# Transposes of the identity placed before waits of TensorE in a linear-attention and mixture-of-experts kernel

## The chip, the cores and the metric

The kernel runs on one core of a Trainium2 chip. The metric is the time of one execution on the device, in microseconds (us): the median of three runs of the kernel before is 821.56 us, the runs lie between 821.05 and 823.49 us. The profile is one more execution, taken by the hardware profiler.

## What is computed

The input x has 16 sequences (blocks) of 512 tokens with 128 features. Each passes an attention layer without a softmax, and then a layer of shared and routed experts, cut here to what matters:

```python
q = silu(x @ Wq); k = silu(x @ Wk); v = x @ Wv             # 16 heads of 8
q, k = lrpe(q, theta), lrpe(k, theta)                      # times cos and sin: 16 per head
energy = einsum('bhnd,bhmd->bhnm', q, k) * tril            # causal, no softmax
out = einsum('bhnm,bhmd->bhnd', energy, v) @ Wo
out = layernorm(out * sigmoid(x @ G1 @ G2)) * gamma + beta
x1 = layernorm(x + out)
# router: 2 of 8 experts for each token, at most 1280 tokens an expert
routed = scatter_add(expert(x1[dispatch]) * weight)        # 8 experts, inner size 512
shared = (silu(x1 @ sg) * (x1 @ su)) @ sd                  # inner size 1024
return layernorm(x1 + shared + routed)
```

## The kernel before

The kernel is written with explicit semaphores. Each of the five engines has its own list of instructions, in an order written out by hand, and waits with `need(engine, semaphore, value)` before an instruction. What is queued behind a waiting instruction on the same engine waits too.

Stage 1 (until about 530 us) goes through the 16 blocks. In `step(b, par)` TensorE does the attention of block b and projects the input of block f = b + 1. A block's attention has four parts c of 128 tokens. For each part `energies_and_state(c)` computes q k^T of the 16 heads (L1960) and a partial sum of the state (L1980), and `states_and_out(c)` computes the output of the part before (`from_states` L1920, `attend` L1935). For c = 0 that is the last part of the block before. Between them stand the turning of the input (`input_turned`, L2046), the projections (`project`, L1853 to L1855 by `three`; `values_projected`, L2291 to L2293), the turning of the keys (`keys_turned`, L2069), the output projection (`project_out`, L2261), the turning of x1 (`turn_x1`, L2250), the router's logits (L2270) and positions (L2282 to L2288), and pairs of gate and up products of the shared experts (`shared_gate`, `shared_up`, also through `three`). Blocks -1 to 1 follow `opening` and `first_blocks`, blocks 2 to 11 `with_feed_forward`, blocks 12 to 14 `with_spare_pairs` (12 in an order of its own), block 15 `last_block`. DIRECT and SPARE are 10. `spare_turn` gives s0 = 2, s1 = 3 for block 13 and s0 = 4, s1 = 5 for block 14.

The other engines follow TensorE. ScalarE copies the turned input (`a_xhi`), copies the turned keys out of PB[0] and PB[1] into Kt (L891, semaphore `a_kt`, two for each block) and the attention's output into oT (L810, `a_out`), and computes silu. VectorE masks the energies into EM (L1243, two instructions for each part, `v_mask`) and the states into SM (L1252, `v_S`), multiplies gate and up of the shared experts out of UB (L1273, `v_h`), rotates q and k by the angles (`turn`, L1224 or L1235) and adds the shared experts' sums (`v_xs`). SyncE's queue starts, block by block, sixteen copies of Q by head (`q_by_head`, L292), the load of an input (L418), and in blocks 2 to 11 eight copies that double Q and K (`double`, L442 and L444). GpSimd sends the rows to the experts' slots (L626).

PSUM has eight banks of 512 columns: PB[0], PB[1], SBK and UB (all "bank" in the trace), EB2 (energy_banks) and EG2 (energy_and_gate_banks, of which the second is GB).

Stage 2 (from about 553 us) computes the experts. `step(e, par)` of expert 0 begins with `turn_rows(0, 0, (0, 1))`, which waits for the first expert's rows from DRAM (`e_ldx`) and turns them into PB[0] and PB[1] (L2385). `spread_down(AGAIN, ...)` (L2328) is down projection of the shared experts. Stage 3 is the rest of the shared experts and the last layernorm.

Of the kernel before, what the change touches and what calls it, by code (L numbers as in the profile page):

```python
# [55 lines left out]
def build(nc, x, wqk, wvg, g1t, g2, wo, gamma, beta, theta, rwt, rg, ru, rd, sg, su, sd, out):  # L56
# [3 lines left out]
    with ctx:  # L60
# [191 lines left out]
        def need(eng, s, value):  # L252

            if value > 0:
                eng.wait_ge(s, value)
# [1591 lines left out]
        def _(pe):  # L1847
# [52 lines left out]
            def down_back(q, bank):  # L1900
# [3 lines left out]
                    ins = t.transpose(bank[:, P * c:P * (c + 1)], down_T(q)[:, P * c:P * (c + 1)], ident[:])  # L1904
                ins.then_inc(pe_dT, 1)

            def from_states(b, par, c):

                need(pe, a_out, 4 * b + c)
                need(pe, v_mask, 8 * b + 2 * c + 2)  # L1910
                need(pe, v_S, NS * b + 2 * c + 1)
                cols = slice(T * c, T * (c + 1))
                for crossed in (1, 0):
                    for s in (0, 1):
                        k, j = 2 * c + s, (s + crossed) % 2
                        rows = slice(T * j, T * j + T)
                        for half in (0, 1):
                            if k > 0:
                                o = T * half + 32 * j
                                ins = t.matmul(AV2[o:o + 32, s, cols], SM[rows, k - 1, 32 * half:32 * half + 32],  # L1920
                                               QT[rows, par, c // 2, half, P * (c % 2) + T * s:P * (c % 2) + T * (s + 1)],
                                               start=True, stop=False)
                    if crossed:
                        ins.then_inc(pe_sm, 1)
# [15 lines left out]
            def step(b, par):  # L1940
# [78 lines left out]
                def states_and_out(c):  # L2019

                    if c > 0 and core:
                        from_states(b, par, c - 1)
                    elif c == 0 and back:
                        from_states(b - 1, 1 - par, 3)
                    if core:
                        state(c, 0)
                    if c == 1 and shared_turn(b - 1) is not None:
                        down_back(shared_turn(b - 1), UB)
                    if c > 0 and core:
                        attend(b, par, c - 1)  # L2030
                    elif c == 0 and back:
                        attend(b - 1, 1 - par, 3)
# [121 lines left out]
                def with_spare_pairs():  # L2154

                    s0, s1 = spare_turn(b, 0), spare_turn(b, 1)
                    if b == DIRECT + 2:
                        states_and_out(0)
                        down_by_column(shared_turn(b - 1), range(3))
                        input_turned()  # L2160
                        energies_and_state(0)
                        down_by_column(shared_turn(b - 1), range(3, 8))
                    else:
                        input_turned()
                        states_and_out(0)
                        shared_pair(s0, SPARE)
                        energies_and_state(0)
                    project(f, 0)
                    if b == DIRECT + 2:
                        turn_x1(b, par)  # L2170
                        states_and_out(1)
                        project(f, 1)
                        project_out(b)
                        energies_and_state(1)
                        logits(b)
                        states_and_out(2)
                        shared_pair(s0, SPARE)
                        project(f, 2)
                        project(f, 3)
                        energies_and_state(2)  # L2180
                        values_projected(0)
                        values_projected(1)
                        states_and_out(3)
                        shared_pair(s1, SPARE)
                    else:
                        project(f, 1)
                        states_and_out(1)
                        project_out(b)
                        energies_and_state(1)
                        shared_gate(s1, SPARE)  # L2190
                        turn_x1(b, par)
                        shared_up(s1, SPARE)
                        states_and_out(2)
                        logits(b)
                        project(f, 2)
                        energies_and_state(2)
                        project(f, 3)
                        values_projected(0)
                        states_and_out(3)
                        values_projected(1)  # L2200
                    energies_and_state(3)
                    keys_turned()
                    positions(b)
# [173 lines left out]
            def step(e, par):  # L2377
# [25 lines left out]
                def down(n):  # L2403
# [6 lines left out]
                                           wd[:, par, f], start=(f == 0), stop=(f == 3))  # L2410
                    ins.then_inc(e_dn, 1)
                if e == 0:
                    turn_rows(0, 0, (0, 1))
                    spread_down(AGAIN, (2,))
                    turn_rows(0, 0, (2,))
                    spread_down(AGAIN, (3,))
# [75 lines left out]
```

## Time and profile before

| | us |
|---|---|
| median of three runs | 821.56 |
| lowest and highest run | 821.05, 823.49 |
| span of the profiled execution (first to last instruction) | 819.0 |
| TensorE busy in it | 771.5 (94%) |
| VectorE, ScalarE, GpSimd busy | 583.9, 368.2, 415.7 |
| TensorE's clock, mean of what was granted, full speed is 1 | 0.988 |

The profile gives the span of its execution, not its whole time. In the timeline a row merges instructions of one line: start, the time from the first start to the last end, the count, and in square brackets the time that the engine was idle before it with what ended it. "issue" there means that the view names no releaser.

### The profile page before, as it was taken

Reading aid. Unit: us, or ns where it says so; the run is one execution under the profiler, and the core shown is the slowest. Engines: PE = TensorE matmul, PEld = TensorE weight load, DVE = VectorE, ACT = ScalarE, POOL = GpSimd, SP = SyncE. Lnnn points to the kernel's source line nnn. Section 1 sums busy time; section 2 is a strip of 40 time slices with the busy share of each in tenths; the row PEclk is TensorE's granted clock in tenths of the full one; section 3 lists DMA queues with packets and bytes.
Section 4 is the critical chain, followed back from the end, with each engine's and each line's share of the span. In section 5 each row is a group of like instructions: output and inputs, shape, how many; then the busy total and the mean of one; then the engine's idle time right before and its main releaser. Section 6 shows DMA issues by size and latency. Waiting matters only on the chain.

```text
span 819.0 us, 30731 instructions
## 1 busy us (share of the span) xinstructions
PE 771.5 (94%) x12462; PEld 627.2 (77%) x12462; DVE 583.9 (71%) x1865; ACT 368.2 (45%) x802; POOL 415.7 (51%) x395
## 2 busy tenths in 40 slices
PE   5889999999999999999998889899999999999994
PEld 4667777777777777778776677688999989899884
DVE  7488798888888888898868898845444454544674
ACT  6334564646546465564633332223322333323484
POOL 6441243523435243342534555671677778876442
PEclk9999999999999999999999999999999999999997
DMA  4155233231333323233322212114444455433455
GB/s 148 46 174 180 78 92 85 64 93 53 100 76 78 90 57 97 61 86 77 77 64 54 69 34 70 42 53 137 98 87 58 80 98 102 72 52 42 126 151 145
DMA packets 71163, 70.56 MB, mean 86 GB/s; under 512 B 11443, under 2 KB 54250, under 8 KB 71024
## 3 DMA queue, kind: packets, MB, share of 16 engines
q1 hardware_dynamic: 53928, 52.33, 23.2%
q0 software_dynamic: 17024, 16.28, 11.0%
q8 instruction: 99, 1.62, 0.8%
q14 instruction: 40, 0.33, 0.1%
q10 hardware_dynamic: 72, 0.00, 0.0%
HBM read 23.99 MB, written 28.89 MB: 65 GB/s over the span
## 4 chain that ended last, share of the span: by engine, by line
PE 78%; DVE 10%; issue 4%; DMA 3%; SPq 2%; POOL 2%; ACT 1%; POOLq 0%; DVEq 0%; ACTq 0%
PE energy_banks L1935 5%; PE bank L1853 5%; PE energy_and_gate_banks L1853 5%; PE bank L1855 5%; PE bank L1854 5%; PE energy_and_gate_banks L2409 4%; PE bank L2409 4%; PE energy_and_gate_banks L1960 4%; PE energy_and_gate_banks L1855 3%; PE energy_and_gate_banks L1854 3%; PE bank L1894 3%; PE energy_banks L1853 3%; PE energy_banks L1855 3%; PE energy_banks L1854 3%; PE bank L1895 2%
## 5 line engine op out<-in xcount | busy, mean ns | idle before, releaser
L626 POOL DMA_INDIRECT dispatched_rows<-x,slot x128 | 140.0, 1093 | 224.5 <-PE energy_banks L1935 132.4
L760 POOL DMA_INDIRECT summed_rows<-VP,goal_i x80 | 123.8, 1548 | 42.5 <-issue 22.7
L1119 ACT ACTIVATE sq<-energy_banks 128x512 f32<-128x512 f32 (+1 forms) x96 | 50.5, 526 | 120.2 <-PE energy_banks L1855 118.5
L842 ACT ACTIVATE hidden_rounded<-sf 128x512 fp32r<-128x512 f32 x88 | 55.3, 628 | 58.8 <-DVE sf L1273 58.0
L832 ACT ACTIVATE sf<-energy_and_gate_banks 128x512 f32<-128x512 f32 x88 | 52.4, 596 | 62.2 <-PE energy_and_gate_banks L1855 60.8
L1273 DVE TENSOR_TENSOR sf<-sf,bank 128x512 f32<-128x512 f32 x88 | 60.1, 683 | 19.4 <-PE bank L1855 19.2
L1935 PE MATMUL energy_banks<-EM,VP 64*32 64x64 f32 x4096 | 59.1, 225 | 1.1 <-issue 1.1
L1243 DVE TENSOR_TENSOR EM<-energy_and_gate_banks,causal 128x512 f32<-128x512 f32 x64 | 43.9, 686 | 18.7 <-PE energy_banks L1960 18.7
L1853 PE MATMUL energy_and_gate_banks<-xgT_hi,ws_hi 128*128 128x512 f32 x108 | 52.1, 482 | 3.4 <-DVE EM L1243 2.6
L1935 PEld LDWEIGHTS energy_banks<-EM,VP 64*32 64x32 f32 x4096 | 47.8, 105 | 4.2 <-issue 3.2
L1853 PE MATMUL bank<-xgT_hi,ws_hi 128*128 128x512 f32 x108 | 45.9, 425 | 3.7 <-DVE sf L1273 1.4
L1725 DVE TENSOR_TENSOR he<-sq,bank 128x512 f32<-128x512 f32 (+1 forms) x48 | 28.7, 599 | 27.1 <-PE bank L1855 22.2
L1960 PE MATMUL energy_and_gate_banks<-QM,KT 32*64 32x128 f32 x1024 | 44.2, 282 | 3.6 <-issue 1.7
L1960 PEld LDWEIGHTS energy_and_gate_banks<-QM,KT 32*64 32x64 f32 x1024 | 29.1, 132 | 23.9 <-issue 23.5
L1960 PE MATMUL energy_banks<-QM,KT 32*64 32x128 f32 x1024 | 44.6, 283 | 0.6 <-issue 0.6
L1243 DVE TENSOR_TENSOR EM<-energy_banks,causal 128x512 f32<-128x512 f32 x64 | 43.4, 678 | 0.0
L1855 PE MATMUL energy_and_gate_banks<-xgT_hi,ws_lo 128*128 128x512 f32 x108 | 43.0, 398 | 0.0
L1854 PE MATMUL energy_and_gate_banks<-xgT_lo,ws_hi 128*128 128x512 f32 x108 | 42.9, 397 | 0.0
L1855 PE MATMUL bank<-xgT_hi,ws_lo 128*128 128x512 f32 x108 | 42.8, 397 | 0.0
L1854 PE MATMUL bank<-xgT_lo,ws_hi 128*128 128x512 f32 x108 | 42.8, 396 | 0.0
L1980 PE MATMUL bank<-VP,Kt 64*32 64x32 f32 x1792 | 40.5, 198 | 1.1 <-ACT Kt L891 0.8
L1853 PE MATMUL bank<-xgT_hi,we_hi 128*128 128x512 f32 (+1 forms) x92 | 37.5, 408 | 3.7 <-DVE xgT_lo L1205 3.0
(255 smaller groups left out, 2178.4 us busy)
## 6 DMA issues: line engine op xcount, KB each, us to landing
QM<-QT SPq DMA_DIRECT2D x248, 32.0 KB
dispatched_rows<-empty POOLq DMA_DIRECT2D x8, 655.0 KB
QM<-dispatched_rows SPq DMA_DIRECT2D x8, 655.0 KB, 6.2
QT<-sq SPq DMA_DIRECT2D x40, 128.0 KB
KT<-sq SPq DMA_DIRECT2D x40, 128.0 KB
xin<-in_x SPq DMA_DIRECT2D x16, 256.0 KB, 2.9
QM<-summed_rows SPq DMA_DIRECT2D x16, 256.0 KB, 2.8
out_x<-QM SPq DMA_DIRECT2D x16, 256.0 KB, 3.2
```

Source lines behind the costliest of these rows:

```text
L626: g.indirect_dma_start(out=xg_d, out_offset=bass.IndirectOffsetOnAxis(ap=slot[:, n % 2, j:j + 1], axis=0), in_=x1[:, n % 2, j % NC, :], in ...
L760: g.indirect_dma_start(out=sum_d, out_offset=bass.IndirectOffsetOnAxis(ap=goal_i[:, par, t:t + 1], axis=0), in_=ye[:, par, t, :], in_offse ...
L832: a.activation(sf[:, n % SF], GB[:], ACT.Silu).then_inc(a_sf, 1)
L842: a.activation(hs_hi[:, f], sf[:, n % SF], ACT.Copy).then_inc(a_hh, 1)
L1243: v.tensor_tensor(EM[:, c % 2, i].rearrange("p (r h) n -> p r h n", r=2), (EG2, EB2)[i][:, :, 0:4 * T].rearrange("p r (h n) -> p r h n", h=4),
L1273: v.tensor_tensor(sf[:, n % SF], sf[:, n % SF], UB[:], ALU.mult).then_inc(v_h, 1)
L1853: t.matmul(dst, w_hi, x_hi, start=True, stop=False)
L1854: t.matmul(dst, w_hi, x_lo, start=False, stop=False)
L1855: return t.matmul(dst, w_lo, x_hi, start=False, stop=True)
L1935: ins = t.matmul(AV2[32 * j:32 * j + 32, s, cols], VP[keys, par, c, 32 * h:32 * h + 32], EM[keys, c % 2, h % 8 // 4, h % 4 // 2 * 4 + h // ...
L1960: ins = t.matmul((EG2, EB2)[r // 2][T * s:T * (s + 1), r % 2, 2 * T * t2:2 * T * (t2 + 1)], KT[rows, par, t2, P * c + T * s:P * c + T * (s ...
L2409: ins = t.matmul((OB, SBK)[hp][:, P * c:P * (c + 1)], he[:, hp, f, P * c:P * (c + 1)], wd[:, par, f], start=(f == 0), stop=(f == 3))
```

## The change

A new function `keep_busy(n, bank)` on TensorE transposes the 128 x 128 identity n times into the first 128 columns of a bank. No instruction reads the result, and the function increments no semaphore. It is called at eight places of blocks 1, 2, 13 and 14 and at one of stage 2, each time behind a wait for the last reader of the bank's former contents, or where such a wait stands already: 4 transposes in block 1 and 10 in block 2 between `input_turned` and `from_states`; 4 in block 13 and 7 in block 14 at the same place (bank PB[1]); 6 in block 13 and 3 in block 14 between `project_out` and `energies_and_state(1)`; 3 in each of these two blocks between `energies_and_state(1)` and `shared_gate(s1)`; and 10 ahead of the first rows of the first expert (bank PB[0]). These are 50 transposes, and seven waits.

```diff
+            def keep_busy(n, bank=UB):
+
+                for i in range(n):
+                    t.transpose(bank[:, 0:P], ident[:], ident[:])
+
@@ states_and_out(c)
                     elif c == 0 and back:
+                        if b in (1, 2):
+                            need(pe, a_xhi, 2)
+                            keep_busy((4, 10)[b - 1])
+                        elif DIRECT + 2 < b < B - 1:
+                            need(pe, a_kt, 2 * b + 2)
+                            keep_busy((4, 7)[b - DIRECT - 3], PB[1])
                         from_states(b - 1, 1 - par, 3)
@@ with_spare_pairs(), blocks 13 and 14
                         project_out(b)
+                        need(pe, v_h, 8 * SPARE + s0 + 1)
+                        keep_busy((6, 3)[b - DIRECT - 3])
                         energies_and_state(1)
+                        keep_busy(3)
                         shared_gate(s1, SPARE)
@@ stage 2, step(e, par)
                 if e == 0:
+                    need(pe, v_xs, SPARE + 1)
+                    keep_busy(10, PB[0])
                     turn_rows(0, 0, (0, 1))
```

## Rows read from the trace of the kernel before

**Rows 1.** The page's chain that ended last, by engine.

```profile
PE 78%; DVE 10%; issue 4%; DMA 3%; SPq 2%; POOL 2%; ACT 1%; POOLq 0%; DVEq 0%; ACTq 0%
```

**Rows 2.** Stretches: length, busy PE, PEld, DVE, ACT, POOL, granted clock, DMA share, GB/s.

```profile
59.30:62.60 3.30, 3.30 (x53) 2.16 (x54) 1.47 (x6) 0.60 (x1) 0.00 (x0) 0.50 0.19 45
62.70:421.00 358.30, 354.22 (x7085) 269.69 (x7084) 303.76 (x949) 194.85 (x435) 137.53 (x128) 1.00 0.32 85
421.10:424.40 3.30, 3.30 (x9) 2.52 (x9) 0.89 (x4) 0.73 (x2) 2.61 (x3) 0.50 0.27 63
424.50:444.90 20.40, 17.56 (x515) 13.62 (x514) 17.52 (x72) 8.86 (x22) 10.65 (x10) 1.00 0.12 31
445.00:448.30 3.30, 3.12 (x9) 2.57 (x10) 2.65 (x6) 1.18 (x2) 0.99 (x1) 0.50 0.53 158
448.40:810.00 361.60, 346.15 (x3553) 303.10 (x3551) 214.05 (x719) 133.15 (x280) 230.58 (x196) 1.00 0.39 83
```

**Rows 3.** TensorE in order of time, block 13, around the third low stretch.

```profile
431.45 1.09 PE L2069 MATMUL bank<-ident,KT 128*128 128x128 f32 x8
...
434.41 0.38 PE L1920 MATMUL energy_banks<-QT,SM 64*32 64x64 f32 x13 [0.90 <-issue]
...
443.61 0.33 PE L1960 MATMUL energy_and_gate_banks<-QM,KT 32*64 32x128 f32 x2 [1.21 <-issue]
...
445.18 0.80 PE L1853 MATMUL energy_and_gate_banks<-xgT_hi,ws_hi 128*128 128x512 f32 x1 [0.62 <-DVE EM L1243]
...
446.62 1.06 PE L2250 MATMUL bank<-ident,x 128*128 128x128 f32 x4
...
448.67 0.37 PE L1920 MATMUL energy_banks<-QT,SM 64*32 64x64 f32 x11
...
450.77 0.48 PE L1853 MATMUL bank<-xgT_hi,we_hi 128*128 128x512 f32 x1
```

**Rows 4.** TensorE in order of time, the other waits that the change fills.

```profile
36.84 0.43 PE L1920 MATMUL energy_banks<-QT,SM 64*32 64x64 f32 x16 [0.95 <-issue]
...
57.53 0.43 PE L1920 MATMUL energy_banks<-QT,SM 64*32 64x64 f32 x16 [2.03 <-issue]
...
460.50 0.43 PE L1920 MATMUL energy_banks<-QT,SM 64*32 64x64 f32 x16 [1.28 <-issue]
...
469.72 0.33 PE L1960 MATMUL energy_and_gate_banks<-QM,KT 32*64 32x128 f32 x2 [0.48 <-issue]
...
471.30 0.50 PE L1853 MATMUL energy_and_gate_banks<-xgT_hi,ws_hi 128*128 128x512 f32 x1 [0.59 <-DVE EM L1243]
...
473.34 0.36 PE L1920 MATMUL energy_banks<-QT,SM 64*32 64x64 f32 x11
...
475.49 0.48 PE L1853 MATMUL bank<-xgT_hi,we_hi 128*128 128x512 f32 x1
...
554.76 1.09 PE L2385 MATMUL bank<-ident,QM 128*128 128x128 f32 x8 [2.49 <-DMA QM<-dispatched_rows]
```

**Rows 5.** TensorE before the second low stretch, block 12.

```profile
420.62 0.30 PE L1935 MATMUL energy_banks<-EM,VP 64*32 64x64 f32 x4 [0.33 <-issue]
```

**Rows 6.** ScalarE and VectorE in order of time, before the waits in block 13.

```profile
432.15 1.08 ACT L891 ACTIVATE Kt<-bank 128x512 f32<-128x512 f32 x2 [1.47 <-PE bank L2069]
...
441.52 0.67 DVE L1273 TENSOR_TENSOR sf<-sf,bank 128x512 f32<-128x512 f32 x1
...
443.24 0.27 ACT L810 ACTIVATE oT<-energy_banks 128x128 f32<-128x128 f32 x1
```

**Rows 7.** The chain that ended last, 60 to 73 us: start, us, what.

```profile
62.68 0.69 SPq L442
...
64.76 7.26 DMA QT<-sq
...
72.65 0.68 DVE sf L1273
```

**Rows 8.** Stretch in which TensorE did nearly nothing but transposes.

```profile
431.40:434.40 3.00, 1.89 (x28) 1.53 (x18) 3.00 (x10) 2.18 (x5) 1.19 (x1) 1.00 0.21 54
```

## The prediction

> **What bounds the kernel now.** I read the page's chain by engine first [rows 1]: 78% of the 819.0 us lies on TensorE, 10% on VectorE. What slows TensorE for a while is therefore likely to be paid. The change removes no work, so the next view is the granted clock by stretches [rows 2]. From 59 to 810 us TensorE has the full clock (2.4 GHz) except in three short stretches at 0.50 (1.2 GHz): from about 59, 421 and 445 us, each at least 3.3 us long. Work that is all TensorE's costs half of such a stretch, 3.3 / 2 = 1.65 us, so the three can cost 5 us at the most. Block 1's wait and the cold start lie ahead of the first of them, and nothing in the change touches the start.
>
> Then the timeline of TensorE, for what stands before a fall. Before 445 us it is block 13: 1.21 us idle before `energies_and_state(1)` and 0.62 us before the gate product [rows 3]. Before 59 us it is block 2: 2.03 us idle before `from_states` [rows 4]. Before 421 us it is block 12, with a last wait of 0.33 us [rows 5]; the change puts nothing into block 12.
>
> **The fillers' own cost.** All 50 transposes go where TensorE waits. Eight transposes of one line take 1.09 us [rows 3]. With about 0.27 us for the last one to run out, that is (1.09 - 0.27) / 7 = 0.12 us for each further one; four at the low clock take 1.06 us [rows 3], some 0.21 us each with 0.45 us for the last. Against the waits [rows 3, 4]:
> - block 1: 4 x 0.12 = 0.5 us in 0.95; block 2: 10 x 0.12 = 1.2 in 2.03.
> - block 13: 0.5 in 0.90, 6 x 0.12 = 0.7 in 1.21, 3 x 0.12 = 0.35 in 0.62.
> - block 14: 7 x 0.12 = 0.8 in 1.28, 0.35 in 0.48, 0.35 in 0.59.
> - first expert's rows: 1.2 in 2.49.
>
> Each fits with 0.1 us or more to spare, so I cost all 50 at nothing. The waits are for other engines or a DMA, which the transposes don't touch; the bank is free. If every cover were gone they would cost 50 x 0.12 = 6.0 us. The trace has no filler before a wait that lasts; the bounds of that are 0 (they hide) and, for the 0.48 us wait of block 14, where the last one's run-out may stick out, 0.35 + 0.27 - 0.48 = 0.14 us. I take 0.
>
> **The seven added waits.** In blocks 13 and 14 the wait for `a_kt` moves ahead of `from_states`. The second copy of the keys in block 13 ends at 432.15 + 1.08 = 433.23 us [rows 6], more than 1 us before `from_states` starts at 434.41 [rows 3]. The wait for `v_h` before `energies_and_state(1)`: the product is done at 441.52 + 0.67 = 442.19 us, while the energies wait for the copy of the output, done at 443.24 + 0.27 = 443.51 [rows 6]. That copy is queued on ScalarE behind `hidden_hi`, which waits for the same product, so the new wait can't become the last. `a_xhi` 2 belongs to the input of block 1, which block 0 already projects; `v_xs` 11 belongs to the sum that `down_back(SPARE, ...)` turned back, which the reloaded and the last round of shared experts follow. Behind each of these waits all of TensorE is queued; all four kinds are due earlier than what comes next. Cost 0; a gain is excluded, since a wait gives nothing back.
>
> **What a kept clock gives, place by place.**
> - Block 13, 445 us. The same instructions, gate to the next `from_states`, run in block 13 at the low clock and in block 14 at the full one: 448.67 - 445.18 = 3.49 us [rows 3] against 473.34 - 471.30 = 2.04 us [rows 4]. The difference is 1.45 us. It isn't given back right behind: from there to the second following projection it is 450.77 - 448.67 = 2.10 us against 475.49 - 473.34 = 2.15. So 1.45 us, on TensorE's own path.
> - Block 2, 59 us. TensorE would be up to 1.65 us earlier. But the chain that ended last doesn't run over TensorE here [rows 7]: it is SyncE's queue, busy with its copies until the doubling of Q starts at 62.68 us, then 7.26 us of that DMA, then VectorE's product at 72.65 us, which stands on VectorE behind the rotation that needs the DMA. The queue doesn't wait for TensorE's late work at 62.68, its copies follow each other. What TensorE wins in block 2 it waits for at 72 us. Bounds 0 and 1.65 us; I take 0.1, since the DMA is the nearer row.
> - Block 12, 421 us. Not touched: 0. It may move, because all before it moves.
> - Block 1 (0.95 us of wait), block 14 (1.28, 0.48, 0.59) and the first expert's rows (2.49) didn't lose the clock in this execution [rows 2, 4]. There the fillers protect what isn't lost: 0 here, up to 1.65 us each in an execution in which the fall lies there.
>
> The sum for this execution: -1.45 - 0.1 = -1.55 us. The profiled span of 819.0 us is 2.6 us under the median of 821.56 us, whose launch and end lie around the span. The runs lie 2.4 us apart (821.05 to 823.49), more than one fall's worth, and a wait of 2.49 us kept the clock where one of 0.33 us came before a fall [rows 4, 5]. So the count and the places of falls very likely differ between executions; I assume the same number on average. **821.56 - 1.55 = 820.0 us.**
>
> **A rule against the change.** Do transposes keep the clock up? From 431.4 to 434.4 us TensorE is busy for 1.89 of 3.00 us; 1.09 us of it are the eight transposes of the keys, four more turn the input, and then it waits 0.90 us. The granted clock is 1.00 there, and the next low stretch begins at 445 us [rows 2, 3, 8]. Before the fall at 421 us no transposes stood, and the wait was only 0.33 us [rows 5]. So the transposes seem to count as activity. The Trainium skill, TensorE: Matmul & The Clock Gate, Part 4: PE-mode transpose, says that for transposes the full clock does not engage, since they don't count as busy in the same way. By that rule the fillers would change nothing, 821.6 us; the stretch of transposes here speaks against it.
>
> **Rivals.**
> - *Two or more falls on the path go.* Besides block 13's, one at the first expert's rows, block 14 or block 1 that other executions have: -1.45 - 1.65 = -3.1 us, 818.5 us; or block 2's stretch counts in full, -1.45 - 1.65, the same. For it: the waits there are long. Against it: none fell in this trace, and the chain [rows 7]. Chance 0.24.
> - *The change doesn't do what it says.* The clock falls as often: because transposes don't hold it, or since the falls land at waits left open (block 12 and others). 821.6 us, from 821.0 to 822.2. For it: the fall at 421 us isn't covered. Against it: rows 8. Chance 0.21.
> - *The fillers stand in the way (slower).* In a wait shorter than its fillers they delay the work behind them. It decides where the wait shrinks below n x 0.12 us, or 0.21 us at the low clock: 3 x 0.21 = 0.63 us is more than the waits of 0.62, 0.48 and 0.59 us. All uncovered: 821.56 + 6.0 - 1.55 = 826.0 us; to be slower by 2.5 us more than two thirds of them would have to be uncovered. Against it: all nine waits are longer now. Chance 0.04.
> - *Forecast*, about one fall's worth on the path, 819.2 to 821.0 us. Chance 0.51.
>
> **How the numbers follow.** The likeliest is 820.0 us. Two and more falls less reach down to 818.2, no effect reaches up to 822.0; the range 818.2 to 822.0 leaves out the slow rival and the tails of both. About 0.3%, or 2.46 us, is what a measurement of this kernel can tell from no change: 819.1 and 824.0 us are the bounds. Faster: nearly all of the first rival and the forecast's lower end, 0.27. Slower: 0.04. Within: 0.69.
>
> **What the profile after would show.** At 57.5, 443.6 and 445.2 us transposes of the identity stand before the waiting instructions, and these start when they did. The granted clock is 1.00 from about 57 us to block 12, and through block 13 and 14. The gate to `from_states` in block 13 takes 2.0 us instead of 3.5. In block 2 VectorE's wait for the DMA before the rotation grows from 0.9 us by what TensorE wins. A low stretch right behind one of the fillers would speak for that rule of the Trainium skill; a fall at 421 us or near it would be expected. Wrong would be: a start of `from_states`, energies or gate later than its releaser by the run-out of a filler; a gain of more than 2 us in a trace in which only blocks 2 and 13 kept the clock, which would mean that block 2's stretch was on the path after all.

## The result, and the profile after

The changed kernel is slower: 827.47 us (median of 6 runs, 824.02 to 829.18) against 821.30 us for the kernel before beside it (6 runs, 819.82 to 823.49), a ratio of 1.0079 with a 95% interval of 1.0057 to 1.0101. The prediction was 820.0 us, with 0.04 on "slower".

The page of the changed kernel, its profiled execution of 827.82 us: the span, the instruction queue of TensorE (q8: packets, MB), and the chain of waits by engine. They answer to [rows 1].

```profile
span 825.8 us, 30831 instructions
...
q8 instruction: 100, 1.64, 0.9%
...
PE 80%; DVE 10%; issue 4%; DMA 3%; POOL 2%; SPq 1%; ACT 1%; POOLq 0%; ACTq 0%; DVEq 0%
```

The windows of TensorE (stretch: length, busy time, instructions, granted clock, share and rate of DMA), which answer to [rows 2]:

```profile
59.00:62.40 3.40, 2.50 (x60) 1.00 0.19 46
421.00:424.40 3.40, 3.40 (x65) 1.00 0.24 56
445.00:448.40 3.40, 3.40 (x144) 1.00 0.54 140
459.00:462.40 3.40, 2.70 (x55) 1.00 0.10 23
491.90:505.50 13.60, 12.96 (x175) 0.50 0.15 44
```

All three low stretches of before are gone, as the change could have made them go. In their place stands one of 13.6 us in block 15, where the change puts nothing. The timeline of TensorE shows the transposes of the identity (L1910) in their waits; these rows answer to [rows 3, 4]:

```profile
430.68 0.60 PE L1910 MATMUL bank<-ident 128*128 128x128 f32 x4
431.66 0.38 PE L1925 MATMUL energy_banks<-QT,SM 64*32 64x64 f32 x13 [0.38 <-issue]
...
55.49 1.26 PE L1910 MATMUL bank<-ident 128*128 128x128 f32 x10
57.50 0.43 PE L1925 MATMUL energy_banks<-QT,SM 64*32 64x64 f32 x16 [0.76 <-issue]
...
558.41 1.25 PE L1910 MATMUL bank<-ident 128*128 128x128 f32 x10
560.52 1.09 PE L2399 MATMUL bank<-ident,QM 128*128 128x128 f32 x8 [0.86 <-DMA QM<-dispatched_rows]
```

In these three waits 0.4 to 0.9 us of idle time is left behind the transposes: they fit. One group of the nine doesn't: the three before `energies_and_state(1)` in block 14.

```profile
466.28 0.28 ACT L810 ACTIVATE oT<-energy_banks 128x128 f32<-128x128 f32 x1
...
467.17 0.49 PE L1910 MATMUL bank<-ident 128*128 128x128 f32 x3
467.59 0.33 PE L1965 MATMUL energy_and_gate_banks<-QM,KT 32*64 32x128 f32 x2
```

The copy that the energies wait for ends at 466.56 us. A stop just before (465.95, below) has made TensorE late, there is no wait left, and the three transposes put off the energies by some 0.4 us (3 x 0.12). The rest of the time goes elsewhere. TensorE's waits from 455 to 505 us, grouped by line and by what ended them (us in total, times, the longest), and its timeline around the last two:

```profile
PE energy_banks L1940 <- issue: 3.8, 2, 2.3
PE energy_banks L1965 <- issue: 1.7, 2, 1.1
PE energy_and_gate_banks L1853 <- DVE EM L1243: 1.0, 2, 0.9
```

```profile
463.43 0.94 PE L1940 MATMUL energy_banks<-EM,VP 64*32 64x64 f32 x62
465.95 0.30 PE L1940 MATMUL energy_banks<-EM,VP 64*32 64x64 f32 x2 [1.58 <-issue]
...
486.97 0.32 PE L1965 MATMUL energy_banks<-QM,KT 32*64 32x128 f32 x2 [1.07 <-issue]
...
489.36 0.92 PE L1940 MATMUL energy_banks<-EM,VP 64*32 64x64 f32 x60
492.54 0.42 PE L1940 MATMUL energy_banks<-EM,VP 64*32 64x64 f32 x4 [2.27 <-issue]
492.89 0.79 PE L1853 MATMUL energy_and_gate_banks<-xgT_hi,ws_hi 128*128 128x512 f32 x1
...
494.34 0.63 PE L1853 MATMUL bank<-xgT_hi,ws_hi 128*128 128x512 f32 x1
494.77 0.63 PE L1854 MATMUL bank<-xgT_lo,ws_hi 128*128 128x512 f32 x1
```

Line 1940 is `attend`: 64 small matmuls in a row, all behind one wait at the head of the group. At 465.95 and 492.54 us TensorE stops *inside* the group, with 62 of 64 and 60 of 64 done, and the profile names no releaser ("issue"). Nothing in the code stands between these matmuls. Behind the second stop the products of 512 columns start 0.43 us apart (494.34, 494.77), which is the low clock; in block 13 of the same trace they start 0.23 us apart.

**What these stops have in common.** I take q8 for TensorE's queue, since its packets match TensorE's instructions in number and in time. The page counts 100 packets on q8, 1.64 MB in all: 16 KB each, one for each 256 of TensorE's some 25,570 recorded instructions (a matmul and its weight load are two; a wait that stands alone is one), so 64 bytes for an instruction. I numbered TensorE's instructions in order of start. In the traces of before and after every stop of over 0.5 us in the middle of a group falls at an instruction number that is 193 over a multiple of 256, that is, at the border between two pieces of 256, and each ends 1.2 to 1.75 us after a 16 KB packet has landed. For the stop that ends at 492.54 us the DMA view of the two stretches before it shows (packets in all; the queues: packets, MB, share):

```profile
DMA packets 0, 0.00 MB, mean 0 GB/s; under 512 B 0, under 2 KB 0, under 8 KB 0
```

from 486.98 to 489.98 us, and

```profile
q8 instruction: 1, 0.02, 6.2%
```

from 489.98 to 491.11 us. So: a border is crossed at 486.97; for 3.0 us no packet moves on any queue; the 16 KB take 1.1 us; 1.4 us later TensorE goes on. The 50 transposes are 100 instructions, 80 of them ahead of block 15. They move every border behind them, and block 15 is dense in small instructions.

**Where the time went.** The same matmul of both traces, counted in order and the transposes of the change left out, starts in the changed kernel later than before by (us, at the time of the trace of before):

```
at         40     45     60     75    415    430    445    455    475    485    505    545    700   end
after   -0.48  +0.96  -0.38  -0.95  -1.26  -2.68  -2.51  -3.96  -2.12  -2.13  +6.74  +6.30  +5.75 +6.80
```

At 455 us the changed kernel is 4 us ahead. It loses 1.8 us by 475 and 8.9 us between 485 and 505: two stops of 1.34 and 2.48 us (from start to start), and what is left, some 5 us, is put down to the low clock that begins in the second of them. The last 1.0 us arises on the other engines, ahead of the store of output in the chain that ended last: that store starts at 810.18 us against 803.42 before.

### The profile page after: what moved, and what is told of

The parts are those of the page before. It is cut to its first block, busy times and chain, and to the rows that moved or that the text cites. A ratio compares the mean times of both kernels' runs of the same rounds, so it can differ in the third digit from the quotient of the medians.

```text
span 825.8 us, 30831 instructions
## 1 busy us (share of the span) xinstructions
PE 779.1 (94%) x12512; PEld 633.2 (77%) x12512; DVE 584.8 (71%) x1865; ACT 368.6 (45%) x802; POOL 415.6 (50%) x395
## 3 DMA queue, kind: packets, MB, share of 16 engines
q8 instruction: 100, 1.64, 0.9%
## 4 chain that ended last, share of the span: by engine, by line
PE 80%; DVE 10%; issue 4%; DMA 3%; POOL 2%; SPq 1%; ACT 1%; POOLq 0%; ACTq 0%; DVEq 0%
PE energy_banks L1940 6%; PE bank L1853 5%; PE bank L1855 5%; PE bank L1854 5%; PE energy_and_gate_banks L1853 5%; PE energy_and_gate_banks L2423 4%; PE bank L2423 4%; PE energy_and_gate_banks L1965 4%; PE energy_and_gate_banks L1855 3%; PE energy_and_gate_banks L1854 3%; PE bank L1894 3%; PE energy_banks L1853 3%; PE energy_banks L1855 3%; PE energy_banks L1854 3%; PE bank L1895 2%
## 5 line engine op out<-in xcount | busy, mean ns | idle before, releaser
L1940 PE MATMUL energy_banks<-EM,VP 64*32 64x64 f32 x4096 | 60.1, 227 | 4.4 <-issue 4.3
L1940 PEld LDWEIGHTS energy_banks<-EM,VP 64*32 64x32 f32 x4096 | 48.1, 105 | 8.2 <-issue 7.0
L1965 PE MATMUL energy_and_gate_banks<-QM,KT 32*64 32x128 f32 x1024 | 45.6, 283 | 2.7 <-issue 0.6
L1965 PE MATMUL energy_banks<-QM,KT 32*64 32x128 f32 x1024 | 46.0, 283 | 1.7 <-issue 1.7
L1965 PEld LDWEIGHTS energy_and_gate_banks<-QM,KT 32*64 32x64 f32 x1024 | 29.4, 132 | 23.2 <-issue 22.9
```

Of the source, the lines that this page charges most:

```text
L1940: ins = t.matmul(AV2[32 * j:32 * j + 32, s, cols], VP[keys, par, c, 32 * h:32 * h + 32], EM[keys, c % 2, h % 8 // 4, h % 4 // 2 * 4 + h // ...
L1965: ins = t.matmul((EG2, EB2)[r // 2][T * s:T * (s + 1), r % 2, 2 * T * t2:2 * T * (t2 + 1)], KT[rows, par, t2, P * c + T * s:P * c + T * (s ...
```

## Experiments

Eleven kernels ran, each beside the kernel before on the same chip. **Theory A**: what costs is the 100 instructions, whose pieces of 256 end at other places. **Rivals**: the transposes' work in the array; the added waits; the moved instruction stream costs the same wherever its borders are.

### The same count, without the work

In each wait the transposes are replaced by as many instructions that only test a semaphore which was set long before. (Two tests share one instruction, hence the 4 * n: the trace has 642 lone waits on TensorE against 542, and 25,566 instructions, as the changed kernel.) The transposes' work in the array is left out.

```diff
-                for i in range(n):
-                    t.transpose(bank[:, 0:P], ident[:], ident[:])
+                for i in range(4 * n - less):
+                    pe.wait_ge(c_id, 2)
```

> Leaves out the arithmetic of the fillers: each transpose of the change (two instructions on TensorE) is replaced, at the same place, by two instructions that only wait for a semaphore long reached. So the instruction list has the same length and the same positions as the changed kernel, and TensorE's array does nothing there. Theory A (TensorE's instructions arrive in blocks of 256, and the 100 added ones move the block borders into dense stretches): the same stops at the same instructions as in the changed kernel, 0.5 to 2.5 us each in blocks 14 and 15, and the clock falls as before; 825 to 829 us. Rival B (the transposes themselves delay work, or the clock's behaviour is made worse by them): without them about 821 us.

Measured: 829.57 us (5 runs), ratio 1.0092 (1.0059 to 1.0125), 0.6 us above the range for theory A and far from the rival's 821. Its timeline, the same two groups (L1965, L1940):

```profile
488.41 0.32 PE L1965 MATMUL energy_banks<-QM,KT 32*64 32x128 f32 x2 [1.04 <-issue]
490.80 0.94 PE L1940 MATMUL energy_banks<-EM,VP 64*32 64x64 f32 x60
493.71 0.30 PE L1940 MATMUL energy_banks<-EM,VP 64*32 64x64 f32 x4 [1.97 <-issue]
```

and its windows at the places where the changed kernel kept the clock:

```profile
59.60:63.00 3.40, 3.40 (x55) 0.51 0.19 46
459.00:462.40 3.40, 3.40 (x73) 0.50 0.19 46
```

The loss is there with no work in the array, and the stop falls behind the same 60 of 64 matmuls. The transposes' work is cleared as the main cause; their number is not. The windows say the other half: with empty waits the clock falls at 59.6 and at 459.0 us; with the transposes in them it is 1.00 at both places. The profiled execution of this kernel was the shortest of its five, 823.26 us, and shows no long low stretch in block 15. That would fit with the low clock behind the stops being the larger part of the loss, when it comes, but it isn't shown: the other four executions (828.09 to 830.98) have no trace.

### Parts of the change

`experts_only` keeps the 10 transposes before the first expert's rows, which stand behind block 15; `blocks12_only` keeps those of blocks 1 and 2 (28 instructions), `blocks1314_only` those of blocks 13 and 14 (52). The edit of the first:

```diff
                         if b in (1, 2):
-                            need(pe, a_xhi, 2)
-                            keep_busy((4, 10)[b - 1])
+                            pass
                         elif DIRECT + 2 < b < B - 1:
-                            need(pe, a_kt, 2 * b + 2)
-                            keep_busy((4, 7)[b - DIRECT - 3], PB[1])
+                            pass
...
-                        need(pe, v_h, 8 * SPARE + s0 + 1)
-                        keep_busy((6, 3)[b - DIRECT - 3])
                         energies_and_state(1)
-                        keep_busy(3)
```

> Only the ten transposes ahead of the first expert's rows stay; all other fillers and their waits are out. Theory A: in stage 1 all borders lie as before, so no new stops; a gain only in executions that would lose the clock at 555 us; 819.5 to 821.5 us. Rival B (transposes delay work): ten of fifty fillers, about a fifth of the loss, 822.5 us.

> Only the fillers of blocks 1 and 2 (14 transposes, 28 instructions, and their two waits). Theory A: the borders of TensorE's list stand 28 instructions later from block 3 on, about where shift32 had them, so the difference to before after block 3 is about -1.3 us and block 15 loses 1 to 2 more than before: 819.5 to 822.5. Rival (the stop in block 15 comes from how early TensorE arrives there, and not from where the borders are): no low clock in block 15 here, and the loss is absent, 819.0 to 820.3; if block 2's fill were itself the cause, 824 or more.

> Only the fillers of blocks 13 and 14 (26 transposes, 52 instructions). Theory A: the borders stand 52 instructions later in block 15; from before's spacing of instructions, pieces would take under 3.9 us, and TensorE stop, near 464 (0.6 us) and 488 (1.5 us); the loss of the changed kernel (a stop of 2.5 us and a low clock behind it) is there in part or not at all: 819.5 to 825. Rival (each of the fillers costs its share of the changed kernel's loss): half of +6.2, 822.5 to 825.5, with no stop over 1 us at a border.

Measured: 819.57 us, ratio 0.9987 (0.9968 to 1.0006); 818.81 us, 0.9980 (0.9957 to 1.0004); 820.70 us, 1.0002 (0.9973 to 1.0030). The second lies 0.7 us below its range, the others in theirs. That it is near its rival's 819.0 to 820.3 doesn't speak for the rival, whose sign was no low clock in block 15: its trace has a stop of 1.50 us there, at 486.46, and a low stretch of 3.4 us from 488.2. None loses, and the parts don't add up to the whole: 1.0079 isn't the sum of three ratios near 1. For costs that each belong to one filler that is a contradiction. For borders it is what one expects, since the instructions before block 15 count together.

### The borders moved by small matmuls in the opening

`shift32` is the kernel before with 8 small matmuls (32 instructions) in the opening. `change_shift32` and `change_shift144` are the changed kernel with 8 and 36 of them.

```diff
             pe.wait_ge(c_id, 2)
+            for _ in range(8):
+                t.matmul(UB[0:32, 0:64], ident[0:64, 0:32], ident[0:64, 0:64], start=True, stop=True)
```

> The kernel before, with 8 small matmuls (32 instructions) into an unused bank at the start of TensorE's list, where it waits for the first input. Nothing else changes. Theory A: all block borders lie 32 instructions earlier in the program. From the trace of before, borders would then come within less than 3.9 us of each other ahead of about 420, 464 and 488 us; new stops there of 0.5 to 1.5 us each; 823 to 827 us. Rival B: the list's length at the start doesn't matter; 821 us within 1 us.

> The changed kernel with 36 small matmuls (144 instructions) at the start of TensorE's list. Theory A: the borders move again, to places that the trace of before makes the least harmful for this change; the stops in block 15 shrink or go; 819 to 823 us, well below the changed kernel. Rival B: as the changed kernel, 827 us, or slower by the added instructions.

> The changed kernel with 8 small matmuls (some 32 instructions) more in the opening: 112 more than before's by block 15 in place of 80. Theory A: the borders leave the places where the changed kernel stopped for 1.8 and 2.5 us; the stops in blocks 14 and 15 are smaller and the low clock from 491 to 505 is gone: 818.0 to 823.5. Rival (any list with 100 instructions more loses the same, wherever the borders are): 825.5 to 830.0.

Measured: 820.24 us, ratio 0.9996 (0.9970 to 1.0021); 831.91 us, 1.0135 (1.0100 to 1.0169); 828.15 us, 1.0079 (1.0055 to 1.0102). All three lie outside what I expected by theory A, and all three fit the times of the rivals: by the times alone these runs speak against A as I had it, and the last two for a cost of the number of instructions. I had tried to foresee the stops from the times of the instructions in the trace of before, and that failed each time: a stop delays everything behind it and so changes which later piece is short. What did come true, in the traces, is that the stops move. With 144 more instructions blocks 14 and 15 have no stop over 0.3 us and no low clock; the loss is in the opening and in blocks 1 to 3 instead; 4.2 us of it are there by 15 us, behind the added matmuls, which were not free there. With 32 more, the stop behind 60 of 64 matmuls and the low clock in block 15 are gone too, and other stops stand in blocks 13 and 14 (up to 1.83 us), with one of 1.50 us in block 15 at 489.50. Its timeline:

```profile
442.70 0.30 PE L1942 MATMUL energy_banks<-EM,VP 64*32 64x64 f32 x4 [1.58 <-issue]
...
464.06 0.40 PE L1856 MATMUL bank<-xgT_lo,ws_hi 128*128 128x512 f32 x1 [1.44 <-issue]
```

The second one stands between two products of 512 columns, not in `attend`: a border may fall anywhere.

### The waits filled with fewer instructions, and that kernel with its borders put back

`wide_fillers` fills the same nine waits for about the same time with matmuls of the identity against the constant table, 192 to 512 columns wide; 11 matmuls at 4 instructions each, 44 in all, 36 ahead of block 15. `wide_shift44` is that kernel with 11 small matmuls in the opening, so that block 15 stands 80 instructions later, as in the changed kernel.

```diff
-                for i in range(n):
-                    t.transpose(bank[:, 0:P], ident[:], ident[:])
+                for cols in n:
+                    t.matmul(bank[:, 0:cols], ident[:], table[:, 0, 0:cols], start=True, stop=True)
...
-                            keep_busy((4, 10)[b - 1])
+                            keep_busy(((256,), (512, 192))[b - 1])
```

(The other four calls in the same way: (256,) and (448,), (384,) and (192,), (192,), and (512, 192).)

> The changed kernel with the same waits at the same eight places, each filled for about the same time, but by wide matmuls of the identity against the constant table (1 or 2 of 192 to 512 columns, 4 instructions each) in place of 50 transposes: TensorE's list grows by some 44 instructions in place of 100, by 36 in place of 80 ahead of block 15. Theory A (what costs is where the borders of the 256-instruction pieces of TensorE's list fall, as the added instructions move them): in block 15 the borders lie near those of shift32, so no stop of 2 us there and no low clock from 491 to 505; the low stretches at 59, 421 and 445 stay away; 817.5 to 822.0. Rival B (the fillers' work in the array, or the added waits, cost the time, whatever their count): as the changed kernel, 825 to 830.

> wide_fillers with 11 small matmuls (some 44 instructions) more in the opening, where shift32's 8 cost nothing: by block 15 TensorE's list is then 80 instructions longer than before's, as in the changed kernel, and its pieces end at the same instructions of blocks 14 and 15 as there, with the eight waits filled by a fifth of the instructions. Theory A (the loss of the changed kernel hangs on where the borders of the pieces fall in blocks 14 and 15): stops of over 1 us at 466 and 492 come back, mostly with a low clock behind the last; 822.0 to 828.0, slower than before. Rival (wide_fillers won because its fills are fewer or wider, not because of the borders): 817.0 to 819.5 as wide_fillers.

Measured: `wide_fillers` 817.69 us (12 runs, 816.45 to 820.25), ratio 0.9960 (0.9936 to 0.9983): faster than before, the best of all kernels here. (How much of this is the clock that the fills keep and how much better places of the borders isn't told apart: by the table below `shift32` and `blocks12_only`, at nearly the same shift, come out at 1.000 and 0.998.) `wide_shift44` 831.17 us (6 runs), ratio 1.0107 (1.0076 to 1.0138), 3.2 us above its range. First the timeline of `wide_fillers` in block 15, with both `attend` groups whole:

```profile
488.77 1.19 PE L1940 MATMUL energy_banks<-EM,VP 64*32 64x64 f32 x64
...
495.69 0.86 PE L1940 MATMUL energy_banks<-EM,VP 64*32 64x64 f32 x64
```

Then that of `wide_shift44` (its lines stand 2 further down; the profiled execution, 836.93 us, was the slowest of its six, and the fastest took 827.26), and its window:

```profile
445.32 2.07 PE L2277 MATMUL bank<-wo_s,oT 128*128 128x128 f32 x8 [2.08 <-issue]
...
473.36 0.30 PE L1942 MATMUL energy_banks<-EM,VP 64*32 64x64 f32 x4 [1.75 <-issue]
...
494.65 0.32 PE L1967 MATMUL energy_banks<-QM,KT 32*64 32x128 f32 x1 [1.35 <-issue]
...
497.42 1.15 PE L1942 MATMUL energy_banks<-EM,VP 64*32 64x64 f32 x61
499.95 0.42 PE L1942 MATMUL energy_banks<-EM,VP 64*32 64x64 f32 x3 [1.38 <-issue]
```

```profile
496.10:513.20 17.10, 15.72 (x264) 0.50 0.13 37
```

Eleven tiny matmuls 400 us earlier turn the fastest kernel into nearly the slowest: the stops in `attend` of blocks 14 and 15 are back, and from 496.1 us, between the stop that ends at 494.65 and the one that ends at 499.95, come 17.1 us at the low clock. The fills, their waits and their places are the same in both, and the eleven cost nothing where they stand: at 20 us of the trace of before, the same matmul starts 0.01 us later. So neither the fills nor the added waits are the cause, and the loss falls due at borders far away. The pair doesn't tell the place of the borders from the number of instructions ahead of them, since the eleven change both.

### How fast TensorE gets instructions

`dense_tail` puts 320 matmuls of the smallest kind (640 in the records, with as many weight loads) behind TensorE's last work. `tail_waits` holds TensorE in it once at the start and then about 20, 60, 120 and 180 instructions behind four borders, with 4 copies on ScalarE each time.

```diff
             stage3(pe, group)
+            for i in range(320):
+                s, j = i // 4 % 2, i % 4
+                t.matmul(PB[s][32 * j:32 * j + 32, 0:64], ident[64 * s:64 * s + 64, 0:32],
+                         ident[64 * s:64 * s + 64, 0:64], start=True, stop=True)
```

The edit of `tail_waits` beside that, on TensorE and at the end of ScalarE's list (each matmul ahead of a wait signals `t_p`):

```diff
+            held = {0: 1, 23: 2, 97: 3, 176: 4, 255: 5}
...
+                if i in held:
+                    pe.wait_ge(t_a, 4 * held[i])
...
+            for k in range(5):
+                if k:
+                    act.wait_ge(t_p, k)
+                for dst in (sf[:, 0], sf[:, 1], sq[:, 0], sq[:, 1]):
+                    a.activation(dst, zeros[:].unsqueeze(1).broadcast_to([P, 4, P]), ACT.Copy).then_inc(t_a, 1)
```

> The kernel before with 320 small matmuls (64 rows, 32 columns of weights, 64 columns moved; about 4 instructions each, so some 1280, five pieces of 256) behind TensorE's last work, where nothing waits for them but the end. It measures by itself how fast TensorE gets new instructions. Theory A: one piece of 256 takes 4 to 6 us however short its instructions are, with a stop of 1 us or more at each of the five borders, each ending 1.2 to 1.8 us after a 16 KB fetch has landed. Rival (the fetch of instructions keeps up with TensorE, and the stops in the middle of groups have another cause): 256 instructions take what their spacing inside a group gives, 2.5 to 3.5 us, with no stops at the borders.

> dense_tail with TensorE held in it: once ahead of the first of the 320 matmuls and then some 20, 60, 120 and 180 instructions behind the first four borders, each time until ACT has made four copies of 512 columns for it (2.3 to 2.8 us with the signals). It asks why some fetches start 1.1 us after their border and others 3 to 4 us. Theory W (TensorE asks for its next piece only when it has read on to some place behind the border, and a wait that stands in between holds the request back): behind the first border, with the wait 20 instructions on, the 16 KB fetch starts over 3 us after the border, some 1.1 us after the wait ends, and behind the wait at 180 it starts 1.1 to 1.7 us after the border, while TensorE is being held; the waits at 60 and 120 say where the place is. Rival (the request goes out at the border, and late fetches are late for a reason outside TensorE): all four start 1.1 to 1.8 us after their border, whatever waits.

Measured: 823.46 us and 839.99 us (one run each; their times say nothing, the tail is added work). The timeline of `dense_tail`:

```profile
804.20 1.83 PE L2466 MATMUL bank<-ident 64*32 64x64 f32 x164
808.54 1.80 PE L2466 MATMUL bank<-ident 64*32 64x64 f32 x128 [2.51 <-issue]
812.29 2.04 PE L2466 MATMUL bank<-ident 64*32 64x64 f32 x128 [1.94 <-issue]
816.03 2.04 PE L2466 MATMUL bank<-ident 64*32 64x64 f32 x128 [1.70 <-issue]
819.50 1.58 PE L2466 MATMUL bank<-ident 64*32 64x64 f32 x92 [1.43 <-issue]
```

This is the mechanism by itself, and somewhat faster than the 4 to 6 us that I expected for a piece: 128 matmuls with their 128 weight loads run in 1.8 to 2.0 us, then TensorE stands for 1.4 to 2.5 us, again and again, after exactly 256 instructions. A piece takes 3.75, 3.74 and 3.47 us from start to start, whether its work takes 1.8 or 2.0. The granted clock isn't what holds it: it is 1.00 up to 809.1 us, over the longest of these stops, and 0.50 from 809.3 us on. The DMA view of 813.34 to 814.48 us has the packet that the start at 816.03 waits for, 1.55 us after its landing:

```profile
q8 instruction: 1, 0.02, 6.2%
```

The fetch of each of these pieces starts 1.1 to 1.7 us after the border before has been crossed. In `tail_waits` TensorE is held for 9.45 us with a piece that landed at 794.69 in hand, and the next 16 KB start only at 819.42, behind the next border. So only one piece is fetched ahead. The Trainium skill, Runtime: NRT & Kernel Launch, section Instruction fetch mechanics, has the blocks of 256 instructions and the fetch of the next one during the current one; the trace agrees with both. It calls the cost of a border "mostly hidden": true for most borders here, and not in this tail, where every border costs 1.4 to 2.5 us. No fixed length of a piece divides the two: in the changed kernel TensorE ran over a border after a piece of 3.02 us (at 418.66 us) without a stop, and stopped after 4.86 us of work (480.77 to 485.63), because the fetch had begun 3.9 us behind the border.

`tail_waits` was to say why some fetches start 1.1 us behind their border and others, as in block 15, 3 to 4 us. My theory (a wait a little way behind the border holds the request back) fell: the four fetches start 0.72, 0.82, 0.71 and 0.72 us after their borders, with TensorE held 20, 60, 120 or 180 instructions further on, and no start of a piece was late. (A wait nearer to the border than 18 instructions wasn't tried; at 480.77 us in the changed kernel two lone waits stand 2 and 4 instructions behind it.) Its timeline has only the waits that I put there:

```profile
818.21 0.95 PE L2474 MATMUL bank<-ident 64*32 64x64 f32 x46 [9.45 <-ACT sq L1175]
821.44 2.36 PE L2474 MATMUL bank<-ident 64*32 64x64 f32 x148 [2.28 <-ACT sq L1175]
826.08 2.47 PE L2474 MATMUL bank<-ident 64*32 64x64 f32 x158 [2.28 <-ACT sq L1175]
```

### All kernels side by side

Worked out from the profiled execution of each: instructions added ahead of block 15; the sum of the stops of 0.2 us or more at borders in blocks 13 to 15 (430 to 521 us), and the longest; the low clock there; how much the kernel fell back against before from 430 to 520 us (the same matmul in both); and the measured ratio.

```
kernel            added   stops (longest)   low clock   fell back   ratio
wide_fillers        36     0.4  (0.42)        3.4         0.0       0.996
blocks12_only       28     2.8  (1.50)        3.4         0.9       0.998
experts_only         0     1.2  (0.60)        3.4        -0.5       0.999
shift32             32     2.8  (1.26)        none       -0.1       1.000
before               0     0.5  (0.53)        3.4          -        1
blocks1314_only     52     2.6  (1.26)        none        1.0       1.000
changed kernel      80     8.0  (2.48)       13.7         9.0       1.0079
change_shift32     112     8.5  (1.83)        none        4.4       1.0079
same_count          80     5.0  (2.19)        3.4         4.4       1.0092
wide_shift44        80     9.3  (2.29)       20.5        13.5       1.0107
change_shift144    224     0.3  (0.30)        none       -2.2       1.0135
```

But for the last, which stops in blocks 1 to 3 (6.7 us from 30 to 80 us, and 10.2 us at the low clock), the four kernels with 5 us of stops or more are the slow ones, and the six with less than 3 us are not slower than before. Each row is one execution, while the ratio is of all: `same_count` is shown by its fastest and `wide_shift44` by its slowest.

One rival is left by the times: the six kernels with 0 to 52 instructions more ahead of block 15 lose nothing, and the five with 80 and more all lose. Against it stands only what the traces show: the time goes at borders and in the low clock near them, and with 224 more, block 15 is free of stops. No run adds one whole piece of 256, which would put every border back where it was with the longer list, or as many instructions behind block 15.

## Why the prediction was wrong, step by step

- **The fillers' own cost, 0 us: the step that failed.** By time it nearly held: behind the transposes of blocks 2 and 13 and of the first expert's rows 0.4 to 0.9 us of idle is left, and one group of three in block 14 delayed the energies by some 0.4 us, because a stop ahead of it had used up its wait. That is the sign of being wrong that I had named, at 467.59 us. But I priced them only as time in a wait. An instruction has a second price, its place in the list, and it falls due far from where it stands. The bounds (0 to 6.0 us if every cover were gone) didn't contain this, since it is no cover. What the runs showed in its place: +9.0 us from 430 to 520 us of the profiled pair, by stops at the borders of pieces of 256 instructions (8.0 us of them, 0.5 before) and some 5 us by the low clock, less what the kept clock gave back and what fell into waits; and the same loss with the transposes' work taken out (`same_count`, 829.57 us).
- **The seven added waits, 0 us: held,** as far as the runs show. They are also in `wide_fillers`, which is faster than before.
- **Block 13, -1.45 us: right in place and size.** The difference between the two traces goes from -2.51 us at 445 to -3.96 at 455, and the window at 445 us has the full clock.
- **Block 2, -0.1 us: the sign was right.** The window at 59 us has the full clock. From 40 to 75 us the difference goes from -0.48 to -0.95 us, with a stop at a border at 45.57 us in between (1.56 us against 0.2 in before). In before such stops stand at 45.8 and 49.4 us (0.74 and 0.88). How much of the difference is the clock isn't told apart; it lies within my bounds.
- **Block 12, 0 us: missed, in my favour.** There is no fall at 421 us in the changed kernel. Of the kernels of the experiments only `tail_waits` has one near it, at 424.4 us. `dense_tail`, which is the kernel before up to 804 us, kept the clock at 421 and at 445 us, and ran 3.35 us ahead of the profiled execution of before at 800 us. So the falls at 421 and 445 us are not properties of the kernel before, only of that one execution. The one at 59 us is more than that: the three traces of that list have it (59.2, 58.3 and 59.2 us), and so do `shift32` and `same_count` (58.6 and 59.6). The prediction said that places and counts very likely differ, and then priced one execution's falls as if they were the average.
- **The rule against the change was rightly not followed.** The reading of [rows 8] holds: with the transposes the clock was kept at 59 and at 459 us, and with as many idle instructions it fell at 59.6 and at 459.0. By that rule of the Trainium skill (TensorE: Matmul & The Clock Gate, Part 4: PE-mode transpose) it should have fallen in both; the measurement decides against it here, at these two places and with one execution of each. It doesn't show that a fall is prevented and not put off: `blocks12_only` and `change_shift32`, with the same transposes, have theirs at 64.9 and 65.1 us.
- **The rivals.** The slow one (fillers longer than their waits, 826.0 us) lies near the measured time by accident; its mechanism was hardly at work. It gave 0.4 us of its kind, in block 14. None of my rivals had the instruction stream as a resource. I had the means: [rows 5] show an idle time of 0.33 us "<-issue" between matmuls of one group in block 12, which no semaphore explains. I read it as a short wait ahead of a fall of the clock. It is a border, 1.6 us after the landing of a packet. The 99 packets on q8 stood on the page too.
- **Chances.** 0.04 for slower was far too little for an edit that shifts everything behind it. That the gain was at most two falls out of a spread of 2.4 us between runs was seen.

What stays open: why the fetches in block 15 start 3 to 4 us after their border when others start after 0.7 to 1.2 us (not the traffic: there was none in one such stretch; not a wait 18 or more instructions behind the border: `tail_waits`). Why the low clock near a stop lasts 3.4 us in one place and over 13 in another, or doesn't come, is open too; that the stop causes it is argued from their standing together. Whether the loss hangs on where the borders fall, as I hold, or on how many instructions are added, is not decided by the times. And where a shift will put the stops: of the forecasts for a moved stream three missed the direction (`shift32`, `change_shift144`, `change_shift32`), and `blocks12_only` and `wide_shift44` came out 0.7 and 3.2 us beyond their ranges. I can read from a trace where the stops are, but not tell it beforehand.

## What to carry to other kernels

Where one engine bounds the kernel with short instructions, count instructions as well as microseconds: divide its list into pieces of 256 and look for "issue" stops inside groups that have no wait. Where instructions are short the engine can stop at the end of a piece (after 1.8 to 2.0 us of work in the tail, after 3.1 and 4.9 us in block 15), and an insertion moves all pieces behind it. If a wait has to be filled, fill it with few wide instructions (here 44 in place of 100: 0.9960 against 1.0079, though `wide_shift44` with the same fill has 1.0107), and before judging such an edit move the stream by a few dozen instructions in the opening: if the time changes as much, it was the borders that were measured. One profiled execution doesn't say which falls of the clock belong to the kernel; another one's windows do.

## What the runs showed of the hardware

- TensorE's instructions arrive 256 at a time in packets of 16 KB that take 0.9 to 1.8 us, one piece ahead (`dense_tail`, `tail_waits`); 1.2 to 1.75 us pass from the landing to the first instruction of the piece where TensorE waits for it. At full demand that is one piece in 3.5 to 4.0 us, or 64 to 74 instructions per microsecond (`dense_tail`).
- Near a stop of 1.4 to 2.3 us in dense work 13.6 or 17.1 us at the low clock can begin (changed kernel, `wide_shift44`), though TensorE is busy for over 90% of these (12.96 of 13.60, 15.72 of 17.10). Most falls lasted 3.4 us; `tail_waits`, whose list up to 804 us is that of before, has one of 13.7 us at 59.2 us, so a long one needs no change to the list. Not every stop is followed by one: 1.97 us in `same_count` was not.
- The same list stops at the same borders from one execution to another, but not for the same time (at 464.78 us in before for 0.53 us, at 462.25 in `dense_tail` for 0.36), and its falls of the clock differ in place and length; the kernel before alone ranged from 816.86 to 825.98 us in 29 runs on one chip.
